# Attention over pairs: key tiles in swapped halves, diagonal quarters of two head groups in one score tile

## What is computed

```python
B, T, C = x.shape                      # 2, 1025, 64
HD = 2;  H = C // HD                   # 32 heads
qkv = x @ w_qkv.T;  q, k, v = jnp.split(qkv, 3, axis=-1)
q = _rmsnorm(heads(q), qn_w);  k = _rmsnorm(heads(k), kn_w);  v = heads(v)
att = jnp.einsum('bhtd,bhsd->bhts', q, k) * scale
causal = jnp.tril(jnp.ones((T, T), bool))
att = jax.nn.softmax(jnp.where(causal, att, -1e30), axis=-1)
y = jnp.einsum('bhts,bhsd->bhtd', att, v)
return y.transpose(0, 2, 1, 3).reshape(B, T, C) @ w_proj.T
```

## Time and profile before

| | |
|---|---|
| median of 3 executions | 1415.05 us (1402.74 to 1417.5) |
| the profiled execution, its own time | 1408.72 us |
| its span in the trace | 1406.9 us |
| mean granted TensorE clock over the span | 0.848 |
| starts of the first and the last exponential of `pairs_attend` | 652.1 and 919.4 us of the span |

### The profile page before, as it was taken

How to read it: one execution, slowest core, us unless ns; L and a number is a source line. 1 busy time by engine, 2 the same in 40 slices (tenths; PEclk the granted TensorE clock), 3 DMA queues, 4 the chain that set the end, 5 groups by cost and what they waited for, 6 DMA issues and landing times. The chain is left out here.

```text
span 1406.9 us, 27739 instructions
## 1 busy us (share of the span) xinstructions
PE 1082.8 (77%) x11399; PEld 620.2 (44%) x11399; DVE 890.9 (63%) x1928; ACT 764.2 (54%) x1071; POOL 139.2 (10%) x163
## 2 busy tenths in 40 slices
PE   6667974562879869945999999989799999997240
PEld 3456963351534444431333333354555566665220
DVE  0476537967891177775675555454788998974524
ACT  0452322231207643358999999932488997982020
POOL 0005401410001200000000000010000000000524
PEclk9788975775659979976999999978899999998575
DMA  7100000021000000000000000010000000002021
GB/s 147 29 1 1 4 4 17 0 34 44 3 0 2 1 0 1 1 2 3 1 2 1 1 1 1 2 24 18 1 2 2 2 3 2 2 2 68 14 45 27
DMA packets 42740, 18.23 MB, mean 13 GB/s; under 512 B 37930, under 2 KB 41564, under 8 KB 42360
## 3 DMA queue, kind: packets, MB, share of 16 engines
q1 hardware_dynamic: 40888, 15.39, 5.2%
q0 software_dynamic: 1728, 1.08, 0.4%
HBM read 12.95 MB, written 3.48 MB: 12 GB/s over the span
## 5 line engine op out<-in xcount | busy, mean ns | idle before, releaser
L2476 ACT ACTIVATE pt_PT<-ps 128x1024 f32<-128x1024 f32 x288 | 266.1, 1108 | 5.9 <-PE ps L2546 5.6
L3459 DVE TENSOR_SCALAR da_AD<-da_QH,da_XG,da_XH 128x1024 f32<-128x1024 f32 x296 | 219.8, 808 | 29.8 <-PE ps L3588 28.8
L3507 ACT ACTIVATE da_AD<-ps,da_NX 128x1024 f32<-128x1024 f32 x214 | 221.2, 1132 | 30.4 <-PE ps L3588 29.9
L3588 PE MATMUL ps<-da_AD,dw_win 128*32 128x256 f32 x4080 | 227.6, 380 | 0.0
L3588 PEld LDWEIGHTS ps<-da_AD,dw_win 128*32 128x32 f32 x4080 | 129.8, 110 | 94.5 <-DVE da_AD L3459 9.7
L2512 PE MATMUL ps<-pt_PT,pa_V 128*32 128x512 f32 (+3 forms) x1536 | 155.5, 499 | 8.3 <-DVE pt_Yc L2453 3.2
L2460 DVE TENSOR_TENSOR pt_PT<-pt_PT,pt_keep 128x512 f32<-128x512 f32 x128 | 84.2, 689 | 61.3 <-ACT pt_PT L2476 60.2
L2546 PE MATMUL ps<-pt_QT,pt_KT 12*128 12x512 bf16 (+3 forms) x768 | 80.2, 334 | 3.2 <-DVE pt_KT L2418 0.5
L2512 PEld LDWEIGHTS ps<-pt_PT,pa_V 128*32 128x32 f32 x1536 | 38.9, 109 | 64.8 <-issue 63.6
L2085 ACT ACTIVATE mt_act<-ps 128x342 f32<-128x342 f32 (+1 forms) x66 | 30.1, 455 | 54.4 <-PE ps L2140 54.4
L2140 PE MATMUL ps<-mt_XF,ew_w 64*128 64x342 f32 (+1 forms) x132 | 54.6, 498 | 0.8 <-ACT mt_WT L2071 0.8
(11 more groups left out here) (779 smaller groups left out, 2041.7 us busy)
## 6 DMA issues: line engine op xcount, KB each, us to landing
em_xs<-in_x_dram SPq DMA_DIRECT2D x2, 1152.0 KB, 9.3
em_xs<-in_x_dram SPq DMA_DIRECT2D x2, 1024.0 KB, 13.6
cp_xbuf<-ci_zero SPq DMA_DIRECT2D x1, 672.0 KB
cp_XS<-cp_xbuf SPq DMA_DIRECT2D x8, 84.0 KB, 2.2
cp_ybuf<-cp_YS SPq DMA_DIRECT2D x8, 84.0 KB, 2.1
ew_win<-in_L_ffn_w_dram SPq DMA_DIRECT2D x2, 320.0 KB
em_WS<-in_L_tok_W_dram SPq DMA_DIRECT2D x8, 72.0 KB
la_blk<-la_scratch SPq DMA_DIRECT2D x8, 64.1 KB
```

Of the source, the lines that this page charges most:

```text
L2476: nc.scalar.activation(PT[:, n % RING, 2 * i:2 * i + 2, :], ps[:, b0:b0 + 2, :], ACT.Exp, scale=SCALE).then_inc(exp_ok, 1)
L3459: nc.vector.tensor_scalar(AD[:, j % RING], QH[:, b], XG[:, b, s:s + 1], XH[:, b, s:s + 1], ALU.max, ALU.subtract).then_inc(ad_dve, 1)
L3507: nc.scalar.activation(AD[:, j % RING], QA, ACT.Abs, bias=NX[:, b, s:s + 1]).then_inc(ad_act, 1)
L3588: ins = nc.tensor.matmul(o, D.win[:, int(by[j] == "D"), hp, 15 - m:47 - m], AD[:, j % RING, hp], start=False, stop=m == (14 if (k, q) == ( ...
```

## The change

A 128x128 tile on the diagonal needs only its half at or under the diagonal, so of its four quarters of 64x64 one is not needed at all, and before the change its exponential is taken too. The change leaves that quarter out. A key tile with an odd number holds its 64-token halves in swapped order (in `QT` for the queries, in V1 for the values). Then the two *upper* quarters of an even and an odd tile can stand one above the other in the same 64 columns: partitions 0 to 63 hold keys of tile j, partitions 64 to 127 keys of tile j + 1. Such a column block is kind "S", and it is made by two matmuls of 64 columns by 12 rows ("64x64" below: 64 output partitions, 64 columns). Ordinary blocks are kind "K".

- Two groups of heads now share a sequence of `per` = 17 steps (a *pair*, 8 of them): 136 steps, 272 exponentials of 128x1024. Steps in a pair: eight whole steps of 512 columns; four "first" steps (S of 64 columns and K of 448); four "second" steps (K of 192 and K of 320); and one step, SHARED (number 5), which holds what is left of both groups and both chunks, four times (K of 64, S of 64). The second chunk comes first.
- Scores of a unit are issued piece by piece over both heads, not head by head.
- A weight block S is multiplied in two matmuls of 64 columns each, both over all 128 rows: one with tile j of `VZ` and one with tile j + 1. `VZ` is a copy of V1 in which the half that does not belong is zero. POOL fills it with zeros in `pairs_prepare` and copies it at the start of `pairs_attend`.
- SHARED has its own buffer `PX`, and its blocks are multiplied together with the four second steps (6, 8, 14, 16). Its masks are four multiplications of 512 columns; every other masked step now has one: 12 for a pair of groups, where there were 16.
- The copy of q to `QT` is three DVE instructions (256, 128 and 128 columns) in place of one of 512.
- In `pairs_prepare` each odd token tile is multiplied by two matmuls with 64 weight columns in place of one with 128.

```diff
+    def first(c):
+        return [("S", c, 4 * c, 0, 0, 64), ("K", c, 4 * c, 64, 64, 448)]
+    def second(c):
+        return [("K", c, 4 * c + 2, 0, 320, 192), ("K", c, 4 * c + 1, 192, 192, 320)]
+    def rest(c, p0):
+        return [("K", c, 4 * c + 3, p0, 448, 64), ("S", c, 4 * c + 2, p0 + 64, 0, 64)]
+    whole = [[("K", 1, j, 0, 0, 512)] for j in range(4)]
+    ends = [first(1), second(1), first(0), second(0)]
+    SHARED, OPEN = 5, (0, 7, 9, 15)
+    duo = [(0, parts) for parts in whole + ends[:1]] + [(0, None)] + [(0, parts) for parts in ends[1:]]
+    duo += [(1, parts) for parts in whole + ends]
+    KIND = {4: "D", 5: "X", 6: "E", 7: "D", 8: "E", 13: "D", 14: "E", 15: "D", 16: "E"}
+    LOCAL = ({0: ("q", 0), 1: ("q", 1), 2: ("k", 0), 3: ("k", 1), 6: ("y", 0), 7: ("y", 1), 8: ("y", 2)},
+             {9: ("q", 0), 10: ("q", 1), 11: ("k", 0), 12: ("k", 1), 13: ("y", 0), 14: ("y", 1), 15: ("y", 2)})
...
+                        if s == SHARED:
+                            sets = [(i, rest(c, QUARTER[i, c])) for i in range(2) for c in (1, 0)]
+                        for i, some in sets:
+                            for kind, c, j, p0, q0, w in some:
+                                if kind == "K":
+                                    ops.append((o[:, p0:p0 + w], kt[:, 128 * j:128 * j + 128],
+                                                qt[:, 512 * c + q0:512 * c + q0 + w]))
+                                else:
+                                    ops.append((o[0:64, p0:p0 + 64], kt[:, 128 * j:128 * j + 64],
+                                                qt[:, 128 * j:128 * j + 64]))
+                                    ops.append((o[64:128, p0:p0 + 64], kt[:, 128 * j + 192:128 * j + 256],
+                                                qt[:, 128 * j + 128:128 * j + 192]))
...
+                        if kind == "K":
+                            cases = [(V1, tile, q0, w)]
+                        else:
+                            cases = [(VZ, tile, 128 * (j - 4 * c), 64), (VZ, tile + 1, 128 * (j + 1 - 4 * c), 64)]
...
-                    for i in range(2):
-                        u = 2 * n + i
-                        act.wait_ge(s_ps, u + 1)
-                        b0 = 2 * (u % 3)
-                        nc.scalar.activation(PT[:, n % RING, 2 * i:2 * i + 2, :], ps[:, b0:b0 + 2, :], ACT.Exp,
+                    nc.scalar.activation(to, ps[:, b0:b0 + k, :], ACT.Exp, scale=SCALE).then_inc(exp_ok, 1)
...
+                            nc.vector.tensor_copy(to[:, :, 0], src[:, :, 0])
+                            for r in range(2):
+                                ins = nc.vector.tensor_copy(to[:, :, 1, r], src[:, :, 1, 1 - r])
...
+                        if u < 8 and i:
+                            for r in (64, 0):
+                                ins = nc.tensor.matmul(o[64 - r:128 - r], XT[:, c0 + r:c0 + r + 64], WT[:], start=True,
+                                                       stop=True)
```

More of the change, by code:

```diff
@@ L100, in constants @@
     c["c_causal"] = (t >= s).astype(np.float32)
-    c["c_keep"] = np.triu(np.ones((128, 128), np.float32))
+    upper, full = np.triu(np.ones((64, 64), np.float32)), np.ones((64, 64), np.float32)
+    c["c_keep"] = np.block([[upper, upper, full, upper], [full, upper, upper, full]])
     for n in (8, 32):
@@ L2210, in _ @@
                 nc.gpsimd.memset(V1[:], 1.0).then_inc(ones_ok, 1)
+                nc.gpsimd.memset(VZ[:], 0.0).then_inc(ones_ok, 1)
             @block.vector
@@ new lines, in weigh @@
+                def weigh(n, parts, bh, start):
+                    for k, (kind, c, j, p0, q0, w) in enumerate(parts):
+                        tile = (bh // 8) * 8 + j
+                        if kind == "K":
+                            cases = [(V1, tile, q0, w)]
+                        else:
+                            cases = [(VZ, tile, 128 * (j - 4 * c), 64), (VZ, tile + 1, 128 * (j + 1 - 4 * c), 64)]
+                        for src, t, to, width in cases:
+                            for q in range(4):
+                                v0 = 3 * (4 * (bh % 8) + q)
+                                ins = nc.tensor.matmul(ps[32 * q:32 * q + 32, 6, to:to + width],
+                                                       src[:, t, v0:v0 + 32], weights(n, q)[:, p0:p0 + width],
+                                                       start=start and k == 0, stop=False, skip_group_check=True)
@@ L2531, in attend @@
+                    if s in OPEN and n:
+                        pe.wait_ge(y_sb, 2 * bh + (s in (7, 15)))
+                    ins = weigh(n, parts, bh, s in OPEN)
+                    if KIND.get(s) == "E":
+                        c = parts[0][1]
+                        ins = weigh(d * per + SHARED, rest(c, QUARTER[odd, c]), bh, False)
                     ins.then_inc(av_ps, 1)
@@ L2535, in _ @@
                     turn(*t)
[L2536 to L2552 removed]
+                step = 0
+                for u in range(len(units)):
+                    for n, q in units[u]:
+                        d, s = divmod(n, per)
+                        if s in (0, SHARED, 9) and q in (0, 2):
+                            pe.wait_ge(turn_sb, number[2 * d + (s > 0), "k", 1] + 1)
+                    if u >= SLOTS:
+                        pe.wait_ge(exp_ok, u - SLOTS + 1)
+                    scores(u)
+                    while step < N and last[step] == u:
+                        if step >= 2 and (step - 2) % per != SHARED:
+                            attend(step - 2)
+                        for t in turns_at(step):
+                            turn(*t)
+                        step += 1
+                for n in range(N, N + TAIL):
+                    if n - 2 < N:
                         attend(n - 2)
```

238 lines of the change are left out of this document (142 added, 96 removed).

## The result

| | before | after |
|---|---|---|
| median | 1414.24 us (1402.74 to 1417.5, 5 executions) | 1437.64 us (1430.88 to 1440.3, 5 executions) |
| ratio, 95% interval | | 1.0179 [1.0145, 1.0213] |
| profiled execution, its span | 1408.72, 1406.9 us | 1430.88, 1429.1 us |
| `pairs_prepare`, first to last instruction | 604.1 to 646.4: 42.3 us | 596.3 to 644.7: 48.5 us |
| `pairs_attend` | 646.6 to 926.2: 279.6 us | 645.0 to 950.5: 305.5 us |

The kernel is 23 us slower, where I forecast 11. The time lies inside the stated range, but the forecast had only half of the change, and most of the other half comes from something that it put at nothing: the clock.

A forecast was written before the change was run, and what follows sets the result against it. ACT's exponentials bound the attention, the bound passing to PE in nine steps of 17. Attention 9.5, copies of q 0.3 and projections 1.0 made 11 us slower: 1420 us profiled, median 1426 us, range 1411 to 1438.

The forecast's parts named there:

- the clock: In the attention over pairs: granted clock taken as 1.00 throughout, with no term for any fall.
- ACT's 1.81 us as floor: In the attention: one exponential starts every 0.90 us, so a step of two costs at least 1.81 us.
- the steps' sum: Over the 17 steps of a pair: 34.5 us against 33.2 before; 10 us more for eight pairs, 9.5 taken.
- The 0.10 us for a change of shape: On PE: each change of the array's shape costs 0.10 us, above 0 and below 0.14.
- values of 704 columns: In second steps with their share of SHARED: five pieces, 1.38 us on PE.
- 576: Values of a first step: 576 columns in three pieces, 1.15 us on PE.
- Rival A: In the scores: changes of shape cost nothing, 8 us faster, 1407 us; chance 0.12.
- B: In the attention: PE is hidden, ACT's floor everywhere, 19 us faster, 1396 us; chance 0.03.
- C: In values and scores: each joint 0.03 us, S pieces one by one, 20 + 1.3 us, 1436 us; chance 0.20.
- rival D: In the attention: granted clock falls; ten us lower cost about 10, 1436 us; sign below 1.00 after 665 us; chance 0.03.
- masks are off the path: On DVE in the attention: 12 multiplications of 0.69 us in place of 16 change nothing; DVE idles 61 us before them.
- the projections, 1.0 us: In `pairs_prepare`: split odd tiles add 0.2 us a round, making DVE 0.6 to 1.5 us late; 1.0 taken.

The follow-up runs named there:

- e9: The changed kernel with the 128-wide score pieces split into two 64-wide ones in the first steps only: 1426.58 us, ratio 1.0086.
- e8: The changed kernel with the 128-wide score pieces split into two 64-wide ones in the SHARED step only: 1410.73 us, ratio 0.9989.
- e10: The kernel before, with SHARED's sequence of mixed-shape pieces added ahead of both units of one step a pair: 1431.75 us, ratio 1.0157.
- e11: The kernel before, with the same extra pieces as e10 but sorted by shape: 1413.7 us, ratio 1.002.
- e6: The kernel before with one extra matmul of 128 keys by 512 columns ahead of each unit of scores: 1423.78 us, ratio 1.0073.
- e4: The changed kernel with each odd tile's projection in one 128-wide matmul, halves not swapped (part of the function changed): 1444.09 us, ratio 1.0267.
- e5: The kernel before with one extra matmul of 64 keys by 64 columns ahead of each unit of scores: 1470.62 us, ratio 1.04.
- e12: The changed kernel run a second time, unaltered, for a second profile: 1436.14 us, ratio 1.0161.
- e13: The changed kernel with `last_weights` moved to the fourth step of a pair, and the turn using it 17 steps later: 1441.84 us, ratio 1.0222.
- e3: The changed kernel with the same matmuls, sorted by shape in the first and SHARED steps: 1411.38 us, ratio 1.0006.
- e1: The changed kernel with the 128-wide score pieces of first and SHARED steps split into two 64-wide matmuls: 1406.68 us, ratio 0.9972.

## Why the prediction was right and wrong

**Right: PE's work, with some luck in the sum.** With ACT's 1.81 us as floor, the steps' sum gave 34.5 us a pair; 34.68 was measured. Before is 33.25 in its quiet pairs, so the change's work costs 8 x 1.43 = 11.4 us, where the sum had 10 and I took 9.5. The 0.10 us for a change of shape, read from the earlier trace rows, held in SHARED and in the first steps, and values of 704 columns (1.34 us, forecast 1.38) and 576 (1.12, forecast 1.15) were near. Rival A is refuted by the 2.28 us of SHARED, B (30.7 us a pair) and C (20 us over eight pairs, so 35.7) by pair 5.

That the total is so near is luck in part. Taken from exponential to exponential, steps 0, 2, 9 and 11 of pair 5, which I had at the floor, cost 0.9 us more than forecast, and steps 4, 5, 8, 13 and 15 cost 0.8 us less. In those four steps PE waits for VectorE's copy that empties the bank of the outputs, 1.3 us a pair (before: 3.0 us in the whole of 680 to 918 us, 0.4 a pair):

```profile
836.82 0.96 PE L2634 MATMUL ps<-pt_PT,pa_V 128*32 128x448 f32 x8 [0.58 <-DVE pt_Yc L2537]
...
840.90 1.06 PE L2634 MATMUL ps<-pt_PT,pa_V 128*32 128x512 f32 x8 [0.25 <-DVE pt_Yc L2537]
...
855.25 0.96 PE L2634 MATMUL ps<-pt_PT,pa_V 128*32 128x448 f32 x8 [0.21 <-DVE pt_Yc L2537]
...
859.33 1.07 PE L2634 MATMUL ps<-pt_PT,pa_V 128*32 128x512 f32 x8 [0.25 <-DVE pt_Yc L2537]
```

**Wrong: the clock, a term put at nothing.** This is the step that failed. The prediction took full clock for the whole stage and gave rival D, whose own sign (a clock below 1.00 after 665 us) is what the trace shows, a chance of 0.03: "The changes of shape make gaps of 0.1 us only". The falls cost 13.3 us in the stage (before lost 2.2 there), more than the 9.5 us that the forecast had for all of its work. The gaps are as short as it said, but behind sixteen of them in 2.3 us the clock goes to 0.50 in most places, though PE never waited for another engine: e9 against e8 shows it in the changed kernel, e10 against e11 in the one before. I sized the mechanism by the length of a gap, from the earlier trace rows where PE was "never idle for long"; the runs show that how close they stand counts. D's price was too high, too: it took about 1 us for each us at the lower level, and 34 us at 0.50 cost 13.3. The worst stretch of after:

```profile
770.00:774.00 4.00, 4.00 (x64) 1.86 (x64) 1.46 (x3) 3.28 (x4) 0.00 (x0) 1.00 0.01 4
774.00:785.00 11.00, 11.00 (x116) 4.76 (x116) 5.43 (x13) 7.34 (x9) 0.00 (x0) 0.53 0.01 1
```

PE counts as busy in both. Here the Trainium skill had a warning that I didn't weigh (TensorE: Matmul & The Clock Gate, A second HAM failure mode: psum-queue depth-cycling): in a kernel that cycles through PSUM banks, a PE that idles in very short pieces between groups of matmuls swings between the two levels. That page's case is another one and doesn't name changes of shape. The trace here agrees as far as short idle pieces go, with gaps of 0.10 us and a clock of 0.50 behind them.

The stage, by the table: 11.4 us of work; 1.5 for `last_weights` in pair 2 (e8 at full clock: 34.61 - 33.14); for the clock, over 34.68 a pair, 1.5 + 1.7 + 1.4 + 3.8 + 1.6 + 0 + 1.5 + 1.8 = 13.3; less 2.2 that before loses in its own pairs 0 and 1. That is 24.0 of 25.9 us; the other 1.9 lie ahead of the first exponential (6.6 us from the stage's start against 5.5) and behind the last.

**Missed: DVE's place.** The prediction said of DVE only that masks are off the path. It didn't follow what stands ahead of the copy of the outputs in the new order: 1.5 us once, with a fall of the clock behind it, and the 1.3 us a pair above.

**Too small: the projections, 1.0 us.** The step assumed the clock of the earlier trace rows, where before ran them at the upper level for a part:

```profile
608.00:616.00 8.00, 3.85 (x21) 3.41 (x22) 4.31 (x6) 4.38 (x10) 0.00 (x0) 0.50 0.00 0
616.00:624.00 8.00, 6.38 (x39) 5.83 (x37) 4.71 (x7) 6.46 (x23) 0.00 (x0) 0.99 0.00 0
```

After ran them at 0.50, PE and then DVE:

```profile
608.51 1.01 PE L2338 MATMUL ps<-pp_WT,pp_XT 64*128 64x192 f32 x2
609.45 0.90 PE L2335 MATMUL ps<-pp_WT,pp_XT 64*64 64x192 f32 x4
610.28 1.00 PE L2338 MATMUL ps<-pp_WT,pp_XT 64*128 64x192 f32 x2
```

```profile
614.57 0.96 DVE L2227 TENSOR_TENSOR pp_sq<-pa_qk 128x768 f32<-128x768 f32 x1 [9.68 <-ACT pa_qk L2298]
```

A round is 1.77 us. e6, with before's projections at the same level, needs (623.42 - 613.02) / 8 = 1.30:

```profile
613.02 10.61 PE L2329 MATMUL ps<-pp_WT,pp_XT 64*128 64x192 f32 x32
623.42 0.84 PE L2329 MATMUL ps<-pp_WT,pp_XL 64*128 64x192 f32 x2
```

So a round costs 0.47 us more, not 0.20, and `pairs_prepare` 2.7 us more (48.5 against 45.8 in e4, e5 and e6). The remaining 3.5 us of 6.2 between the two profiles are the clock's; whether the change had a part in that is not shown (e4, without the split, had the lower level there too). In the first profile of after 7.8 us came back in the unchanged recurrent stage, at a higher clock there; e12, where `pairs_prepare` had the upper level for a part, has none of that and ended 30.3 us behind before's profile: 1.1 ahead of `pairs_prepare`, 3.5 in it, 25.8 in the attention. The medians, 23 us apart, are the better measure, since before's profiled execution lies 5.5 under its median.

**Open**: why a dense step at one moment costs a stretch of 3 us and at another 7 to 14 (e4, e13), and none in pair 5; why a wait of 2 us in pair 2 is followed by a fall in some kernels and not in e8 and e9; and whether changes of shape do more than the same idle time in another form.

## What to carry to other kernels

Count the changes of the array's shape in a row, not only their sum: each cost 0.10 us, and behind sixteen close together the clock mostly fell too, for 3 us and more. Sort the matmuls of a step by shape, or split the wide ones so that all have one shape: e3 and e1 do after's work and are 24 and 29 us faster, by their ratios. When a sum is made at full clock, ask what the new order does to the clock, and follow the other engines' queues to the copy that frees the bank. A small edit elsewhere can move the falls: the attention took 9.4 us more in e4 and 4.3 in e13. So read the pairs at full clock apart from the rest.

## What the runs showed of the hardware that I had not expected

- An order of matmuls alone, with PE shown as busy, decides whether the granted clock holds: 1.00 in e11, 0.50 behind six of eight bursts in e10.
- 576 changes of shape spread evenly over the stage (e5) left it at 0.99, with one fall of 3 us.
- A fall costs less than its length would say, 1.1 to 1.7 us for one of 3 us (e9, after). That PE goes on at half speed meanwhile, and ACT has something in hand, would explain it; no run tests it.
- One 512-column matmul more per unit (e6), 0.21 us of streaming, took a pair from 33.25 to 34.67 us. A step has two of them, on different rows, and its scores took 0.54 us in place of 0.32: 0.22 us for both, as if they ran side by side. So the 36 of a pair occupy PE for 18 x 0.22 = 4.0 us, of which ACT's floor hides all but 1.42.
